# Twelve weight chunks of a fused attention and expert kernel: low halves by an adding DMA instead of by TensorE

## The reference, cut to what matters

```
x = L0_attn_x                                   # (4, 1024, 256)
h = layernorm(x) * (1 + ca) + sa
q, k, v = unit_projection(h W + b)              # unit modulus of every frequency
x = x + ga * unbind(cumsum(bind(k, v)), q)      # products in the frequency domain
h = layernorm(x) * (1 + cb) + sb
gate = h @ gate_w; top 2 of 8 experts, softmax of the two
y = dense_2(swiglu(dense_1(h)))                 # dense_1_w (8, 1024, 256), dense_2_w (8, 256, 512)
out = x + gb * sum of the two experts' y by weight
```

## Time and profile before

| | |
|---|---|
| median of 3 runs | 595.83 us (595.48, 595.83, 599.93) |
| the profiled execution's own time | 594.5 us |
| its span | 592.5 us |
| mean granted TensorE clock | 0.944 of full |
| busy: PE, DVE, ACT, POOL | 93%, 81%, 50%, 50% |
| block loop | to about 245 us of the span |
| experts' products | from about 290 us |

### The profile page before, as it was taken

One profiled execution on the slowest core, in us unless ns is written; L12 is line 12 of the kernel. 1 busy time (PEld: TensorE's weight loads), 2 busy tenths in 40 slices (PEclk: granted clock), 3 DMA queues, 4 the chain that ended last, 5 costly groups with the idle time before them and its releaser, 6 DMA issues.

```text
span 592.5 us, 13011 instructions
## 1 busy us (share of the span) xinstructions
PE 548.7 (93%) x3955; PEld 407.6 (69%) x3956; DVE 478.2 (81%) x1059; ACT 294.4 (50%) x497; POOL 294.8 (50%) x197
## 2 busy tenths in 40 slices
PE   8998999999999995667999999999999999999992
PEld 6545565555646552526588888888888888888771
DVE  1288979999999989999488888888888888888762
ACT  4776678879696863641533333333333333333330
POOL 0004033432423242000548888888888888887532
PEclk9998989999897977866999999999999999999998
DMA  8333633653745437723567787777777777765722
GB/s 310 121 99 122 184 97 109 191 160 107 212 107 153 125 97 246 289 42 70 144 118 137 143 134 136 131 138 129 139 134 135 141 129 133 130 98 86 113 38 28
DMA packets 81571, 79.32 MB, mean 134 GB/s; under 512 B 44596, under 2 KB 71348, under 8 KB 81272
## 3 DMA queue, kind: packets, MB, share of 16 engines
q0 software_dynamic: 16912, 31.74, 30.2%
q1 hardware_dynamic: 63320, 46.15, 27.5%
q10 hardware_dynamic: 1296, 0.87, 0.5%
HBM read 44.06 MB, written 22.23 MB: 112 GB/s over the span
## 4 chain that ended last, share of the span: by engine, by line
PE 73%; DVE 17%; ACT 3%; issue 3%; DMA 2%; POOL 1%; POOLq 0%; DVEq 0%; ACTq 0%
PE ps L778 31%; PE ps L799 15%; PE ps L530 11%; PE ps L589 4%; DVE region L1258 2%; PE ps L543 2%; PE ps L629 2%; PE ps L625 1%; DMA region<-in_dft 1%; PE ps L600 1%; PE ps L461 1%; PE ps L590 1%; DVE region L1273 1%; DVE region L1380 1%; DMA out_rows<-w_stage,region 1%
## 5 line engine op out<-in xcount | busy, mean ns | idle before, releaser
L778 PE MATMUL ps<-region,w_sb 128*128 128x256 f16 (+1 forms) x1872 | 200.4, 264 | 1.9 <-ACT region L1026 1.3
L778 PEld LDWEIGHTS ps<-region,w_sb 128*128 x1872 | 172.6, 98 | 24.9 <-issue 3.2
L1690 POOL DMA_INDIRECT out_rows<-w_stage,region x71 | 135.7, 1912 | 49.6 <-issue 20.0
L1680 POOL DMA_INDIRECT region<-h_scratch,region x71 | 95.9, 1351 | 71.5 <-DVE region L1539 45.0
L1571 DVE TENSOR_SCALAR region<-ps,region 128x256 f32<-128x256 f32 (+1 forms) x156 | 64.3, 454 | 55.3 <-PE ps L778 53.8
L799 PE MATMUL ps<-region 128*128 x852 | 99.5, 273 | 3.5 <-DVE region L1585 3.3
L1130 ACT ACTIVATE region<-ps,region 128x256 f32<-128x256 f32 (+1 forms) x156 | 62.2, 451 | 79.2 <-PE ps L778 74.2
L1142 ACT ACTIVATE region<-region 128x1024 f16<-128x1024 f32 (+1 forms) x39 | 38.2, 981 | 109.4 <-DVE region L1579 106.8
L799 PEld LDWEIGHTS ps<-region 128*128 128x128 f16 x852 | 82.6, 98 | 14.4 <-issue 4.3
L530 PE MATMUL ps<-region 128*128 128x512 f32 x192 | 84.2, 595 | 3.2 <-ACT region L894 3.2
L1660 POOL TENSOR_TENSOR region<-region 128x512 f32<-128x512 f32 x30 | 37.3, 1270 | 96.2 <-DVE region L1285 96.2
(11 more groups left out here) (229 smaller groups left out, 699.2 us busy)
## 6 DMA issues: line engine op xcount, KB each, us to landing
w_stage<-in_w SPq DMA_DIRECT2D x20, 512.0 KB, 3.8
region<-in_x SPq DMA_DIRECT2D x8, 512.0 KB, 7.5
out_rows<-region SPq DMA_DIRECT2D x8, 512.0 KB, 3.0
h_scratch<-gb_bc SPq DMA_DIRECT2D x4, 1024.0 KB, 6.7
h_scratch<-region SPq DMA_DIRECT2D x8, 512.0 KB, 3.2
region<-region POOLq DMA_DIRECT2D x7, 512.0 KB, 4.6
region<-in_ramp SPq DMA_DIRECT2D x1, 2064.0 KB, 10.6
region<-in_w SPq DMA_DIRECT2D x4, 512.0 KB, 6.0
```

The costliest lines, as they stand in the source:

```text
L778: mm = pe.matmul(ps[:, GV + 2 * half + a, (f % 2) * MT:(f % 2) * MT + wide], w, xg_t[:, s, xa * KD + k, 0:wide], start=(n == 0), stop=(n = ...
L1680: G.indirect_dma_start(out=xg_rows[:, t % XG, u, :], out_offset=None, in_=h_scratch, in_offset=bass.IndirectOffsetOnAxis(ap=gather_idx[:, ...
L1690: G.indirect_dma_start(out=out, out_offset=bass.IndirectOffsetOnAxis(ap=scatter_idx[:, at:at + 1], axis=0), in_=y_sb[:, t % 2, u, :], in_o ...
```

## The change

For chunks 4 to 15 (those of `low_piece(t + 1, ...)` in the passes t = 1 to 6) TensorE no longer makes the low halves. After the high half, ACT overwrites the staged weights with the high half times -1/64 in float32; POOL issues a DMA that adds the weights, read from device memory again, onto the staging tile; and ACT makes the low half with one 1024-wide copy, scaled by 64. The twelve adding DMAs stand on POOL's queue: chunks 4 and 5 behind the DMA of x2 in pass 1, chunks 2t + 2 and 2t + 3 ahead of the DMA of x2 in the passes t = 2 to 6. The items of the removed pieces leave the rotation of the PSUM banks.

```
@@ psum_plan and the loop of TensorE, pass t
-                    low_piece(t + 1, 0)
                     nyquist_cols(t + 1)
...
-                low_piece(t + 1, 1)
+                if t in (-1, LAST):
+                    low_piece(t + 1, 1)
                 if t >= 0:
                     nyquist_sums(t)
                 if t >= 2:
                     gate(t - 2)
-                low_piece(t + 1, 2)
+                if t in (-1, LAST):
+                    low_piece(t + 1, 2)
                 if t >= 0:
                     nyquist_row(t)
-                low_piece(t + 1, 3)
+                if t in (-1, LAST):
+                    low_piece(t + 1, 3)
                 if t >= 0:
                     inverse(t)
@@ ACT
-                    if c == 2 and t >= 2:
-                        low_piece(t, 0)
...
                 nc.scalar.activation(parts_of(n)[HI], staged(n), ACT.Copy, scale=SW).then_inc(w_hi, 1)
+                if summed(n):
+                    act.wait_ge(w_hi, n + 1)
+                    nc.scalar.activation(staged(n), parts_of(n)[HI], ACT.Copy, scale=-1.0 / SW).then_inc(w_neg, 1)
+
+            def low_chunk(n):
+
+                act.wait_ge(w_acc[n % 2], 16 * (n // 2 - 1))
+                nc.scalar.activation(parts_of(n)[LO], staged(n), ACT.Copy, scale=SW).then_inc(w_lo[n % 2], 2)
...
-                low_piece(t + 1, 1)
+                if t in (-1, LAST):
+                    low_piece(t + 1, 1)
+                else:
+                    low_chunk(2 * t + 2)
                 if t >= 2:
                     gate(t - 2)
-                low_piece(t + 1, 2)
+                if t in (-1, LAST):
+                    low_piece(t + 1, 2)
+                else:
+                    low_chunk(2 * t + 3)
...
-                low_piece(t + 1, 3)
+                if t in (-1, LAST):
+                    low_piece(t + 1, 3)
@@ POOL
+            def add_weights(n):
+
+                pool.wait_ge(w_neg, n - 3)
+                G.dma_start(staged(n), source_of(n), accum_op=ALU.add).then_inc(w_acc[n % 2], 16)
+
             for t in range(NBLK):
                 s, b = t % 2, t // 2
                 if t >= 2:
                     pool.wait_ge(all_ready, t + 1)
                     low_rows(t - 2)
+                    for n in (2 * t + 2, 2 * t + 3):
+                        if summed(n):
+                            add_weights(n)
                 if t >= 1:
                     pool.wait_ge(x2_ready, t)
                     G.dma_start(x2, x_sb[:, (t - 1) % XS], accum_op=ALU.add).then_inc(x2_sum, 16)
+                if t == 1:
+                    for n in (4, 5):
+                        add_weights(n)
```

More of the change, by code:

```diff
@@ L92, in psum_plan @@
             continue
-        elif t < NBLK:
+        elif t == NBLK - 1:
             items.append(("lo", t + 1, 0))
-            if t + 1 < NBLK:
-                items.append(("ny", t + 1, 0))
-        if t < NBLK:
+        elif t + 1 < NBLK:
+            items.append(("ny", t + 1, 0))
+        if t == -1 or t == NBLK - 1:
             items.append(("lo", t + 1, 1))
@@ L317, in adaln_moe_kernel @@
         w_lo = sems("w_lo", 2)
+        w_neg, w_acc = sem("w_neg"), sems("w_acc", 2)
         lo_mm, w_hi, gate_split, h2_hi, h2_lo, hid_hi, y_mid = (sem(n) for n in (
@@ L368, in load_weights, with summed, pieces_to, source_of @@
             sp.dma_start(staged(n), src).then_inc(w_in[stage_of(n)], 16)
+        def summed(n):
+            return 4 <= n < 2 * NBLK
+        def pieces_to(t, i):
+            return 4 * (t if t < 2 else t - NBLK + 2) + i + 1
+        def source_of(n):
+            at = (n if n < W1_CHUNKS else W2_ORDER[n - W1_CHUNKS]) * WCH
+            return (w1 if n < W1_CHUNKS else w2)[:, at:at + WCH]
         def parts_of(n):
@@ L979, in low_piece @@
                     act.wait_ge(tp_done, KD * NBLK)
-                act.wait_ge(lo_mm, 4 * t + i + 1)
+                act.wait_ge(lo_mm, pieces_to(t, i))
                 nc.scalar.activation(parts_of(2 * t + i // 2)[LO][:, (i % 2) * BLK:(i % 2 + 1) * BLK],
```

## The result

| | before | after |
|---|---|---|
| median of 3 runs | 595.83 us | 612.87 us (611.99, 612.87, 615.55) |
| the profiled execution's own time | 594.5 us | 611.99 us |
| its span | 592.5 us | 610.2 us |
| mean granted TensorE clock | 0.944 | 0.900 |

The kernel became slower: the ratio is 1.0269, with an interval from 1.0218 to 1.0319. The forecast was 601.3 and its range ended at 612.0; the measured median lies just above it.

The account below looks back on a forecast made before the run. TensorE and DVE were level, with DVE's waits capping the gain; x2's chain, 23.4 + 2.1 copies + 2.0 clock + 0.6 transfers = 28.1 us a block against DVE's 25.3, gave 601.3 us, range 590 to 612.

Parts of the forecast that it names:

- What bounds the kernel: Block loop: TensorE and DVE are level, so removing TensorE work gains at most DVE's waits, 6.1 us in all.
- The way of x2: Chain from DVE's moments through ACT and TensorE to x2's DMA landing: lengthens from 23.4 to 28.1 us, past DVE's 25.3.
- Two copies: On ACT ahead of the copy to x2: each block's copies back add 2.1 us, bounds 1.9 and 2.3.
- The clock: TensorE's inverse, passes 1 to 6: starts at clock 0.50 and ends 2.0 us late, bounds 1.0 and 4.0.
- The transfers: DMA engines: weight adds still under way delay x2's landing by 0.6 us a block, bounds 0 and 1.2.
- The wait of the low halves: On ACT: adds land some 5 us before DVE's moments, low halves come after those, so waiting is free.
- The sum: Whole kernel: 28.1 us a block, pass 2's landing at 102.8, pass 7's moments 5.8 us late, 601.3 us.
- rival 2: Block loop: the x2 chain stays hidden and DVE's waits go, 5.1 us off, 590.4 us; chance 0.12.
- rival 1: TensorE's inverse: the clock costs nothing on the x2 chain, 26.1 us a block, 591.3 us; chance 0.22.
- Rival 3: Block loop: all added terms at their upper bounds, 30.9 us a block, 20 late, 615 us; chance 0.13.

Follow-up runs that it names:

- The removal alone: The changed kernel without the copies back and without the adding DMAs, low halves of chunks 4 to 15 wrong: 595.46 us, ratio 0.9993 to the kernel before.
- the writing DMAs: The changed kernel with its twelve weight DMAs writing instead of adding, low halves of chunks 4 to 15 wrong: 600.79 us, ratio 1.0127.
- the first run with twelve products: The changed kernel plus twelve unused float16 products on TensorE ahead of the Nyquist row in passes 1 to 6: 603.36 us, ratio 1.0129.
- the removal with four groups of them: Neither copies back nor adding DMAs, with five unused products in each of the four places of the removed pieces: 596.96 us, ratio 1.0023.
- the first rearranged kernel: Complete changed kernel; high halves and copies behind the copy to x2, adds behind x2's DMA, low halves behind the roots, twelve products: 608.38 us, ratio 1.0223.

## Why the prediction was right and wrong

**What bounds the kernel: right, as far as the runs go.** No run gained more than DVE's waits of 6.1 us, whatever was taken from TensorE. The removal alone gives 0.9993, and its best form, with the low rows cut short, 0.9949.

**The way of x2 becomes the bound: right.** L1251 waits for its DMA in five passes, and DVE's own work doesn't set the pace from pass 2 to pass 6. The prediction had 2 to 3 us a wait; it was 4.0 to 5.2.

**Two copies, 2.1 us a block: right.** From L894 of the spectra to the issue of x2's transfer it was 173.23 - 165.50 = 7.73; in after it is 189.51 - 179.60 = 9.91, 2.2 more.

**The clock, 2.0 us a block: right in kind, a little too high.** Against 3.1 warm, the five passes have 0.6 to 2.0 more, 1.5 on average. The Trainium skill (TensorE: Matmul & The Clock Gate, What's actually happening) has activity release the throttle. The trace agrees as far as the cold inverse goes, 1.19 against 0.67 for L643's pair. What I had not thought of is that the lateness moves POOL's work onto DVE's.

**The transfers, 0 to 1.2 us, taken as 0.6: this is the step that failed.** It measured 7.6 to 8.5 us from issue to landing where I had 5.1 (4.5 and 0.6): 2.8 a block on average of the last four. I took the spread of x2's landings as the bound, and reasoned only that "the second weight add is still under way". I didn't ask how long one such transfer fills all the engines. The trace of before held the answer. Windows of before, around the x2 add that was issued at 147.07 and landed at 151.60, with nothing else under way:

```profile
147.00:148.00 1.00, 1.00 (x3) 0.38 (x2) 1.00 (x2) 0.95 (x2) 0.89 (x1) 1.00 0.00 0
148.00:149.00 1.00, 1.00 (x4) 0.46 (x3) 0.96 (x2) 0.97 (x2) 0.00 (x0) 1.00 0.67 131
149.00:150.00 1.00, 1.00 (x4) 0.49 (x3) 1.00 (x2) 0.81 (x2) 0.00 (x0) 1.00 1.02 197
150.00:151.00 1.00, 1.00 (x3) 0.38 (x2) 1.00 (x2) 0.16 (x1) 0.00 (x0) 1.00 1.04 197
```

One add fills all sixteen engines for some 2.7 us (0.67 + 1.02 + 1.04), and is through about 4.0 us behind its issue. The windows of before from 144 to 147 have shares of 0.03, 0.98 and 0.48 for the write of L422 (L436 in after): 1.5 us. In after this write is issued at 154.50, the adds at 154.54, 156.57 and 159.72, and the engines begin at about 155.5. By the rows of before they have 1.5 + 3 x 2.7 = 9.6 us to do, until 165.1, where x2's add alone would be through at 163.7: 1.4 us, more than twice my 0.6 and above my upper bound. Measured, the shares of after from 155 to 167 add up to 10.3 (2.9 for an add), the engines are busy until 166, and the landing follows 1.5 us behind that, where it followed 0.6 behind in before. That is the rest up to 3.2 in this block, and why the landing comes later behind the last full window I can't say. The Trainium skill (DMA: Bandwidth & Descriptors, Issuing engines are not separate DMA queues) says that DMAs from all issuing engines run on the same sixteen DMA engines; it gives no time for it. The windows agree: with a write of SyncE (154.50) and the first adds of GpSimd under way, the share is 1.06 at its height (156 to 157), no higher than with adds alone (1.05 to 1.09).

**The wait of the low halves, taken as free: wrong in the first pass.** The add for chunk 5, issued at 73.94, landed 9.8 us later, and ACT waited for it ahead of the Nyquist row. It isn't x2's add that holds it up, which had landed at 70.0: SyncE issues the write of x2, a transfer of 1024 KB (L420) and the load of x from 70.0 to 71.0, and the DMA share is 0.86 to 1.17 from 71 to 83. The prediction had looked at what the adds do to x2, and not at what SyncE's transfers do to the adds. Timeline of ACT in after:

```profile
83.82 1.06 ACT L996 ACTIVATE w_sb<-w_stage 128x1024 f16<-128x1024 f32 x1 [1.99 <-DMA w_stage<-in_w]
84.78 0.57 ACT L1055 ACTIVATE region<-ps 1x512 f32<-1x512 f32 x1
```

It costs 2.0 us once. From pass 2 on the wait is free, as I had said.

**The start, 1.7 us, not foreseen and not the change's.** Pass 1's bind starts at 62.06 for 60.33. Timelines of TensorE, the rows of the modulation (L507 in after, L493 in before), ahead of anything that was changed:

```profile
30.23 5.29 PE L507 MATMUL ps<-region 128*4 128x512 f32 x8
```

```profile
29.52 3.60 PE L493 MATMUL ps<-region 128*4 128x512 f32 x8
```

The instructions are the same; the clock of 27 to 35 us was granted at 0.79 in after and at 1.00 in before. It isn't the change's doing as such. After and its twelve variants all have these instructions unchanged; in the profiled executions of the writing DMAs, of the first run with twelve products, of the removal with four groups of them and of the first rearranged kernel they take 3.60 us, and in the other nine 5.27 to 5.29. So a comparison of two of these runs can hold 1.5 to 1.8 us that belong to neither. What decides it I don't know.

**The sum.** Pass 2's moments at 108.81 for 102.8 forecast: 6.0, of which 1.7 for the start, 2.0 for the low half and 2.6 for the landing, less 0.4 for the clock (1.6 for 2.0). The landing counts from 5.5 here, since the forecast for pass 2 started from a landing that had taken 5.5 (101.69 - 96.17), and it took 8.1. Then four blocks of 29.85 for 28.1: 7.0, from 2.8 more for the landing, 0.5 less for the clock, and half a microsecond less elsewhere on the way, which no row here explains. The last block, in which DVE sets the pace, took 22.96 for 23.2 forecast. In all 6.0 + 7.0 - 0.2 = 12.8, and 5.8 + 12.8 = 18.6.

**The rivals.** The way of x2 hidden (rival 2) and a clock that costs nothing (rival 1) are both excluded by the rows above. Rival 3, "all at the upper bounds" with 30.9 a block, came nearest with 29.85, by the term of the transfers and not by that of the clock. It had 0.13 and lay outside my range by half; a bound for the transfers from the windows above would have put more weight there.

**What stays open.** Whether some order of a complete version beats before. The best is level. What the waits point to is an order with no products ahead of the Nyquist sums and with POOL's low rows away from DVE's multiply; no run tried both. What sets the clock at the start of the kernel, and with it 1.7 us, stays open too.

## What to carry to other kernels

A transfer added to a way that others share is priced by how long it fills the DMA engines, times the number that are not yet through when the important one is issued, and not by its landing time when alone. Work taken from an engine is worth the waits for that engine and no more, and the pieces removed may have been what kept its clock up; look where its next large products start. When one chain comes later by a microsecond or two, look which instructions of DVE and POOL now lie on top of each other.

## What the runs showed of the hardware

A multiply of DVE with two inputs (128x516 float32) takes 0.70 us alone, and 2.01 to 2.26 when a subtraction on POOL (2.13 us) is under way at its start; POOL's keeps its 2.13. With POOL's instruction cut to 0.31 us it is 0.70 again. The Trainium skill (SBUF — State Buffer, Who interferes with whom) says that the two engines share a port pair, that it is an exclusive lock, and that a DVE instruction with two SBUF inputs contends with a GpSimd instruction that reads SBUF. The trace agrees: at 120.55 DVE starts 0.67 behind POOL, whose instruction ends at 122.01, and DVE's ends 0.55 after that. In the other three passes it ends 0.55 or 0.56 behind POOL's too, and 0.54 in pass 6 of before, where it took 0.88.

A plain transfer of 512 KB takes POOL 0.55 to 0.59 us to issue and an adding one 0.85 to 0.89, and they differ more in how long they keep the DMA engines: 1.6 us against 2.7 to 2.9. Where adds fill them, they move 197 to 217 GB/s. The plain ones ahead of x2's add cost its landing nothing that can be seen: 4.5 to 5.2 us, and 4.5 to 5.0 in the run without them.
